# A two-layer FFN block on one core: in its Strassen stages one copy on ScalarE, one subtraction on VectorE and one weight sum on GpSimd change place

## The reference

```python
def _anemll_linear(x, w, su, sv):
    w_eff = w * (su @ sv)                      # su: (out, 4), sv: (4, in)
    return jnp.einsum('bsh,oh->bso', x, w_eff)
a = _anemll_linear(x, gate_w, gate_su, gate_sv)   # 512 -> 1792
b = _anemll_linear(x, up_w, up_su, up_sv)         # 512 -> 1792
d = jax.nn.silu(a) * b
return _anemll_linear(d, down_w, down_su, down_sv)  # 1792 -> 512
...
x = x + _L0_ffn_ref(_L0_cond_ref(x, ...), ...)    # cond: gate/up, silu, down, with adapters per sample
x = x + _L1_ffn_ref(_L1_cond_ref(x, ...), ...)    # linear with adapters, then an int4 ffn
```

## Time and profile before

| what | us |
| --- | --- |
| median of 3 runs | 627.49 (627.46 to 629.29) |
| the profiled execution | 627.37 |
| its span, on which the trace's clock runs | 625.8 |
| PE busy | 616.5 |
| DVE busy | 451.9 |
| ACT busy | 315.6 |
| POOL busy | 243.3 |
| the two Strassen stages with the down phase between, in the trace | 212.93 to 398.79 |

### The profile page before, as it was taken

How to read it: one execution, slowest core, us unless ns; L and a number is a source line. 1 busy time by engine, 2 the same in 40 slices (tenths; PEclk the granted TensorE clock), 3 DMA queues, 4 the chain that set the end, 5 groups by cost and what they waited for, 6 DMA issues and landing times.

```text
span 625.8 us, 8105 instructions
## 1 busy us (share of the span) xinstructions
PE 616.5 (99%) x2950; PEld 499.9 (80%) x2950; DVE 451.9 (72%) x546; ACT 315.6 (50%) x418; POOL 243.3 (39%) x198
## 2 busy tenths in 40 slices
PE   8999999999999999999999999999999999999996
PEld 6788888788778888788878878888788888788885
DVE  4575464543548999885347897645779998999987
ACT  5675514343634444443014444334657887478860
POOL 3680010000000006851024566430004889948896
PEclk9999999999999999999999999999999999999999
DMA  8740022101021111411201101152222221222103
GB/s 253 185 149 29 25 87 88 66 17 31 21 74 65 37 34 52 151 59 60 67 23 78 54 15 34 63 108 68 81 71 98 64 82 39 102 69 84 66 1 135
DMA packets 24474, 45.19 MB, mean 72 GB/s; under 512 B 9972, under 2 KB 12020, under 8 KB 24372
## 3 DMA queue, kind: packets, MB, share of 16 engines
q1 hardware_dynamic: 21972, 40.80, 20.9%
q0 software_dynamic: 2176, 3.36, 2.0%
q10 hardware_dynamic: 288, 0.52, 0.2%
HBM read 40.74 MB, written 2.10 MB: 68 GB/s over the span
## 4 chain that ended last, share of the span: by engine, by line
PE 86%; DVE 9%; issue 2%; DMA 1%; ACT 1%; SPq 0%; DVEq 0%
PE ps_down L1926 7%; PE ps_down L1928 7%; PE ps_down L1927 7%; PE ps_up L1926 4%; PE ps_up L1927 4%; PE ps_up L1928 3%; PE ps_gate L1926 3%; PE ps_gate L2113 3%; PE ps_m L2113 3%; PE ps_gate L1927 3%; PE ps_m L2114 3%; PE ps_gate L2114 3%; PE ps_gate L1928 3%; PE ps_up L2113 3%; PE ps_down L2113 3%; PE ps_down L2114 3%
## 5 line engine op out<-in xcount | busy, mean ns | idle before, releaser
L830 POOL TENSOR_TENSOR act_lo<-up,act_hi 128x512 fp32r<-128x512 f32 x14 | 19.0, 1361 | 183.0 <-ACT act_hi L1116 181.7
L1926 PE MATMUL ps_down<-act_hi,w_hi 128*128 128x512 f32 (+1 forms) x180 | 70.7, 393 | 0.0
L1927 PE MATMUL ps_down<-act_lo,w_hi 128*128 128x512 f32 (+1 forms) x180 | 70.2, 390 | 0.0
L1928 PE MATMUL ps_down<-act_hi,w_lo 128*128 128x512 f32 (+1 forms) x180 | 70.1, 389 | 0.0
L871 POOL TENSOR_TENSOR up_sum<-up_sum,up_more 128x1024 f32<-128x1024 f32 x14 | 33.7, 2407 | 62.5 <-DVE up_more L1481 62.5
L1355 DVE TENSOR_TENSOR w_lo<-w_raw,w_hi 128x512 fp32r<-128x512 f32 (+4 forms) x41 | 40.3, 982 | 14.7 <-ACT w_hi L943 10.1
L943 ACT ACTIVATE w_hi<-w_raw 128x1024 fp32r<-128x1024 f32 (+4 forms) x30 | 27.0, 899 | 43.8 <-PE ps_down L1928 17.9
L1926 PEld LDWEIGHTS ps_down<-act_hi,w_hi 128*128 128x128 f32 (+1 forms) x180 | 33.8, 188 | 7.2 <-issue 0.4
L1928 PEld LDWEIGHTS ps_down<-act_hi,w_lo 128*128 128x128 f32 (+1 forms) x180 | 33.8, 188 | 7.2
L1927 PEld LDWEIGHTS ps_down<-act_lo,w_hi 128*128 128x128 f32 (+1 forms) x180 | 33.8, 188 | 6.6
L1481 DVE SCALAR_TENSOR_TENSOR gate_sum<-ps_up,s_group,gate_sum 128x1024 f32<-128x1024 f32 x28 | 35.8, 1280 | 4.0 <-PE ps_up L2114 4.0
(11 more groups left out here) (302 smaller groups left out, 1793.3 us busy)
## 6 DMA issues: line engine op xcount, KB each, us to landing
w_int<-in_ffn_gu SPq DMA_DIRECT2D x14, 512.0 KB, 3.5
w_raw<-in_cond_gu SPq DMA_DIRECT2D x9, 512.0 KB, 3.4
w_raw<-in_ffn_gu SPq DMA_DIRECT2D x9, 512.0 KB, 3.5
w_raw<-in_ffn_dn SPq DMA_DIRECT2D x8, 448.0 KB, 3.1
w_int<-in_ffn_dn SPq DMA_DIRECT2D x8, 448.0 KB, 3.1
xp<-in_x SPq DMA_DIRECT2D x8, 256.0 KB, 5.3
w_raw_third<-in_ffn_gu SPq DMA_DIRECT2D x4, 512.0 KB, 3.5
xp<-in_x SPq DMA_DIRECT2D x1, 2048.0 KB, 9.4
```

The costliest lines, as they stand in the source:

```text
L1926: nc.tensor.matmul(ps[0:m, :], w_hi[0:r, s, cols], rhs_hi(k, r), start=start and n == 0, stop=False)
L1927: nc.tensor.matmul(ps[0:m, :], w_hi[0:r, s, cols], rhs_lo(k, r), start=False, stop=False)
L1928: last = nc.tensor.matmul(ps[0:m, :], w_lo[0:r, s, cols], rhs_hi(k, r), start=False, stop=stop and n == len(ks) - 1)
```

## The change

There are three edits.

- ACT, in the eight tiles named above: `m2_to_sbuf(q)` comes ahead of both `seven_act_hi` of the tile before, and not between them.
- POOL, in tiles q = 3 and 10, where it makes the sums for q = 4 and 11: the third sum (the subtraction, L824) waits until the first two low parts of that same tile's weights are done on DVE.
- DVE, in q = 0: `piece_lo(1, 1)`, the second low part of the weights of tile 1, is issued ahead of tile 0's `part_sum`, and not after it.

```diff
                 nc.gpsimd.tensor_tensor(low[:, 12 * P:14 * P], raw[:, 4 * P:6 * P], raw[:, 6 * P:8 * P], ALU.add).then_inc(w_summed, 1)
+                if before_second(ph, j - 1):
+                    pool.wait_ge(piece_ready, 2 * q + 2)
                 nc.gpsimd.tensor_tensor(low[:, 8 * P:12 * P], raw[:, 0:4 * P], raw[:, 4 * P:8 * P], ALU.subtract).then_inc(w_summed, 1)
...
-                if j > 0:
-                    seven_act_hi(ph, j - 1, 0)
                 if q > 2:
                     m2_to_sbuf(q)
                 if j > 0:
-                    seven_act_hi(ph, j - 1, 1)
+                    for c in range(CH):
+                        seven_act_hi(ph, j - 1, c)
...
                 if q == 0:
-                    piece_lo(ph, 1, 0)
+                    for piece in range(2):
+                        piece_lo(ph, 1, piece)
...
-                if nxt is ph and not before_pair(ph, j) and q != 2:
+                if nxt is ph and not before_pair(ph, j) and q not in (0, 2):
                     piece_lo(ph, j + 1, 1)
```

## The result

| | median us (range, runs) | ratio to before, 95% interval |
| --- | --- | --- |
| before, on the same chip | 627.38 (627.0 to 629.29, 12) | |
| changed | 628.87 (628.59 to 632.68, 12) | 1.0027 [1.0014, 1.0040] |

The change costs 1.49 us in the medians, 0.24%.

The account below looks back on a forecast made before the run. PE, busy 616.5 of 625.8 us, was taken to bound the kernel, so only its waits count. Tile 4 +0.44, tile 11 +0.39 and tile 0 +0.1 gave 627.49 + 0.93 = 628.4 us, range 626.8 to 629.2.

Parts of the forecast that it names:

- The bound, PE's waits alone: PE busy 616.5 of 625.8 us, so only its waits count; four Strassen-stage waits with restarts allow 3.0 us at most.
- The turns of DVE and POOL: Instructions with two SBUF operands exclude each other; the turn passes 0.14 us before the recorded end, to the engine that waited.
- The rival of dearer turns: Tiles 4 and 11: turns handed over later, each delay counting eight times; 630.5 us if 0.12 after the end; 5%.
- the row at 257.89: Old trace, DVE instruction taking 0.67, read as showing that instructions with an operand in PSUM aren't held by POOL.
- Edits 1 and 2 in tiles 4 and 11: Old waits go; new ones of 0.72 at product 5 and 0.78 at product 7 in tile 4; +0.44 and +0.39.
- The turn that I called close: Tile 5's first low part beats POOL's first sum by 0.1 us; otherwise 627.6; 20% together with another turn falling differently.
- the step from the end of `diff` to PE: Tile 4, product 5: `diff` ends at 260.00 and PE starts 0.06 us later, at 260.06.
- Edit 1 elsewhere: Copy first in the other six tiles costs nothing, since PE has no wait for a copy there.
- Edit 3: Tile 0: wins 0.38 at tile 1 but loses it at tile 2, with another slow restart; +0.1, bounds -0.38 to +0.15.
- DVE now waits 0.17 for the rounding: Tile 0: the earlier second low part waits for its rounding, sliding the last sum from 232.61 to 232.78.
- The sum: Whole kernel: 0.44 + 0.39 + 0.1 = 0.93 us slower, passing through to the end; median 628.4 us.
- The full gain of 3.0 us: Rival: the old waits go and none comes, needing early `diff` and silu; 624.5 us; 6%.

Follow-up runs that it names:

- e2: Kernel before with only POOL's third sum of tiles 4 and 11 waiting for the second low part; 631.18 us, ratio 1.0053.
- e6: On e4, DVE makes `diff` ahead of the two products of the tile before in tiles 4 and 11; 628.77 us, 1.0019 to the kernel before.
- e1: Kernel before with only ACT's copy of the first product moved ahead of both roundings; 627.05 us, ratio 0.9986.
- e4: The change without DVE's earlier low part in tile 0, so ACT's copy and POOL's wait only; 628.70 us, 1.0014 to the kernel before.
- e8: Kernel before plus copy first, POOL's next sums before subtractions, third sum waiting for first low part only, DVE's second low part directly behind; 625.21 us, 0.9959.
- e11: The same kernel as e2 run once more to look at the granted clock behind PE's waits; 634.15 us.

## Why the prediction was right, and where its sizes were off

The forecast was 628.4 and the measurement 628.87, in the range of 626.8 to 629.2. The change forecast was +0.93 and the one measured +1.49; 0.42 of the difference is edit 3. By its own steps:

- **The bound, PE's waits alone.** Held: every experiment that moved the time did so with a wait of PE that the trace shows, and e2 with the lower clock behind such waits as well. Not each wait counts: in e6 the one at product 5 is gone and the tile is as long. The 3.0 us given as all that can be won leave out the wait at tile 1, which the step on edit 3 counts.
- **The turns of DVE and POOL.** Held: handed over 0.13 before the recorded end and to the one that waits (L1627 in the rows above: 1.78 forecast 1.75, second `act_lo` 2.01 forecast about 2.0). The rival of dearer turns is refuted. The Trainium skill ("SBUF — State Buffer", section "A bandwidth-pool intuition that's wrong") gives some 115 ns after the end for blocked descriptor writes; that doesn't hold for these pairs, and no run here has such writes. The lock that the Trainium skill has for the whole instruction ("SBUF — State Buffer", section "SBUF: two separate sides") agrees but for those 0.13. One reading was wrong: the row at 257.89 can't show that an operand in PSUM frees DVE from the turn, since POOL had nothing to do from 257.41 to 258.71. What was read from it still holds: `diff` at 259.15 takes 0.69 while POOL works from 258.71 to 259.99, and in the changed kernel 0.68 at 259.69 beside POOL's 1.28 at 259.91.
- **Edits 1 and 2 in tiles 4 and 11.** The waits fell where they were said to: none for the low part or the copy, then product 5 (marked 0.71 and 0.72, forecast 0.55) and product 7 (0.58 and 0.62, forecast 0.6). The turn that I called close, low part ahead of POOL's first sum, went as forecast: the sum took 1.74. Tile 4 is 0.52 longer for +0.44, tile 11 0.49 for +0.39. These 0.08 and 0.10 are in the chain to the silu. PE's last matmul of tile 3 starts 0.32 later than in the trace of before (253.75 against 253.43). Less these 0.32, the second subtraction ends at 258.30 (forecast 258.24), L1627 at 258.85 (258.78), the rounding for tile 5 at 263.24 (263.15), and product 7 starts at 263.77 (263.69), small slips in hand-overs from engine to engine that add up. **Mis-sized** was also the step from the end of `diff` to PE, 0.06 in the forecast and 0.14 in the trace (260.37 to 260.51). The 0.06 came from the earlier trace rows; the earlier trace rows had another case, 0.15 (223.23 to 223.38), and I didn't weigh it. It costs nothing here, since PE waits at product 7 anyway, but it does in edit 3.
- **Edit 1 elsewhere.** Nothing, as said: e1 has no wait of PE in the other six tiles.
- **Edit 3.** Forecast +0.1, came +0.52. The wait at tile 2 in place of tile 1 came as said, and nothing of what tile 1 gave back is left. **The step that failed** is "DVE now waits 0.17 for the rounding" as the only delay: up0 comes 0.38 later, since gate1 was left directly behind `part_sum`, for which it waits. Of the 0.38, 0.18 is the wait for the rounding and 0.20 this neighbourhood. PE also starts 0.14 and not 0.06 behind up0, as behind `diff`. With a restart of 0.12 these are 0.38 - 0.08 + 0.12 = 0.42, where 0.08 is what up0 was early before (20.60 against 19.68 + 0.84). The last 0.1 is the later start of `diff`, 6.12 against 6.01, whose cause stays open; with edit 3 alone it was earlier (5.88), and tiles 0 to 3 took 39.65, 0.29 more than before, which is 0.42 - 0.13.
- **The sum.** 0.93 forecast; 0.52 + 0.49 + 0.52 + 0.09 = 1.62 in the stages and 1.49 in the medians. e4, without edit 3, has 0.52 and 0.48 in the two tiles and -0.02 before them, 1.07 in all and 1.01 in the medians. The full gain of 3.0 us, which I gave 6%, needed both chains to be early; e8 comes near it with 2.4.

## What to carry to other kernels

A wait that protects one engine's turn delays everything that is queued behind the waiting instruction; put it on the earliest event that already gives the turn (here the first low part, once the second stands directly behind it), and move what others wait for (the sums) ahead of what nobody is short of. Where an engine waits twice in a row for two chains, the later chain sets the time, and speeding up the earlier one gains nothing. Edits that are judged together hide each other: here the gain was in one of three and the loss in another. Before two instructions of DVE are made neighbours, look whether the second waits for the first.

## What the runs showed of the hardware

- Waits of 2.04 to 2.09 us on PE were followed by a granted clock of 1.2 GHz in three of four cases (e2 and e11), each costing 1.6 us over about eight matmuls; waits of 0.87 (changed kernel) and 1.74 us (e6) were not, in one profiled execution each. A wait can so cost nearly twice its length, and not in each execution.
- Instructions of DVE and POOL that both have two operands in SBUF held each other up: L1627 took 1.78 for 0.68, POOL's first sum 1.74 for 1.28. The one that waited worked from 0.13 us before the recorded end of the other.
- On DVE, gate1 directly behind `part_sum`, whose result it reads and whose semaphore it waits for, starts 0.79 us behind it, against 0.60 for instructions without such a wait; `part_sum` behind `diff` is 0.72 (before).
- A waiting matmul started 0.14 us behind the recorded end of `diff` and of up0, and 0.05 to 0.06 behind that of the copy, the silu and the low part in tile 4; behind a low part in tile 1 it was 0.15. What decides between the two wasn't found.
